# Cross attention: a finished batch's projection, norms, gate, experts and stores stand up to two slots sooner in the slot tables

## The reference

```
x = layernorm(x + self_attention(x))                       # causal, plus a "memory" term
x = layernorm(x + cross_attention(ctx, ctx, x) @ Wo.T + bo) # keys and values from ctx
x = layernorm(x + ffn(x))
# ffn: logits = x @ gate_w (8 experts), weights = softmax, top 2
#      e0 = silu(x @ w0.T + b0), e1 = silu(x @ w1.T + b1)
#      out = e0 * weight0 where expert 0 is first choice + e1 * weight1 where expert 1 is second
```

## Time and profile before

| | us |
|---|---|
| median of 3 runs | 1775.47 |
| the runs | 1770.29, 1775.82, 1775.47 |
| span of the profiled execution | 1773.4 |
| PE busy | 1681.7 (95%) |
| DVE busy | 1254.6 (71%) |
| POOL busy | 1161.8 (66%) |
| ACT busy | 974.2 (55%) |

### The profile page before, as it was taken

How to read it: one execution, slowest core, us unless ns; L and a number is a source line. 1 busy time by engine, 2 the same in 40 slices (tenths; PEclk the granted TensorE clock), 3 DMA queues, 4 the chain that set the end, 5 groups by cost and what they waited for, 6 DMA issues and landing times.

```text
span 1773.4 us, 30895 instructions
## 1 busy us (share of the span) xinstructions
PE 1681.7 (95%) x10626; PEld 1111.0 (63%) x10626; DVE 1254.6 (71%) x2785; ACT 974.2 (55%) x1939; POOL 1161.8 (66%) x964
## 2 busy tenths in 40 slices
PE   5999999999999989999998999999999999999998
PEld 4766666666666547877863556566565656656566
DVE  5677777777777666767876776877778686777745
ACT  4555555555555443433445565656666665666554
POOL 2556556556555554744565977878788786878874
PEclk9999999999999989999998999999999999999999
DMA  6556555555555464576625543535344354534210
GB/s 199 147 149 168 145 152 156 153 156 165 141 153 153 122 194 152 181 219 185 193 66 155 144 115 88 139 90 155 91 114 114 82 138 99 144 93 108 63 42 31
DMA packets 167273, 237.29 MB, mean 134 GB/s; under 512 B 22087, under 2 KB 73287, under 8 KB 167117
## 3 DMA queue, kind: packets, MB, share of 16 engines
q1 hardware_dynamic: 167116, 235.31, 48.2%
HBM read 91.57 MB, written 41.94 MB: 75 GB/s over the span
## 4 chain that ended last, share of the span: by engine, by line
PE 68%; DVE 12%; POOL 8%; DMA 4%; issue 4%; ACT 2%; SPq 1%; POOLq 0%; DVEq 0%; ACTq 0%
PE bank L1652 9%; POOL cross_added L1974 7%; PE bank L201 5%; PE bank L202 5%; PE bank L203 5%; DVE bank L585 5%; PE bank L1522 5%; PE bank L1490 5%; PE bank L1461 5%; PE bank L369 4%; PE bank L305 4%; PE bank L356 3%; DVE bank L548 2%; PE bank L1558 2%; PE bank L329 2%
## 5 line engine op out<-in xcount | busy, mean ns | idle before, releaser
L1471 DVE TENSOR_REDUCE cross_negmax<-bank 128x1 f32<-128x512 f32 x512 | 338.7, 674 | 149.8 <-PE bank L1461 147.2
L1738 ACT ACTIVATE cpt<-bank 128x512 f32<-128x512 f32 x512 | 297.7, 595 | 143.6 <-PE bank L1490 140.1
L548 DVE CUSTOM_DVE_ANT_0 bank<-bank,future 128x128 f32<-128x128 f32 (+3 forms) x512 | 243.0, 488 | 177.8 <-PE bank L356 177.7
L430 ACT ACTIVATE pt<-bank 128x256 f32<-128x256 f32 (+3 forms) x512 | 217.5, 444 | 260.2 <-PE bank L305 256.1
L1974 POOL TENSOR_TENSOR cross_added<-cross_added,cpt 128x2048 f32<-128x2048 f32 x61 | 280.0, 4591 | 11.5 <-ACT cpt L1738 11.0
L618 POOL TENSOR_SCALAR_AFFINE_SELECT pt<-pt 128x512 f32<-128x512 f32 x128 | 81.1, 634 | 246.8 <-ACT pt L430 246.8
L1490 PE MATMUL bank<-cqk 98*128 98x512 f32 x512 | 227.4, 444 | 7.1 <-ACT cpt L1738 6.2
L1461 PE MATMUL bank<-cqk 96*128 96x512 f32 x512 | 212.5, 418 | 10.7 <-DVE cross_negmax L1471 8.6
L1974 POOL TENSOR_TENSOR cross_added<-cpt,cpt 128x2048 f32<-128x2048 f32 x32 | 146.6, 4581 | 84.0 <-ACT cpt L1738 84.0
L305 PE MATMUL bank<-qk 98*128 98x256 f32 (+2 forms) x512 | 180.6, 359 | 8.4 <-ACT pt L430 3.9
L356 PE MATMUL bank<-qk 96*128 96x256 f32 (+2 forms) x512 | 169.5, 335 | 4.4 <-DMA qk<-stage 4.4
(11 more groups left out here) (207 smaller groups left out, 3623.8 us busy)
## 6 DMA issues: line engine op xcount, KB each, us to landing
qk<-stage SPq DMA_DIRECT2D x384, 128.0 KB, 2.3
cqk<-cstage SPq DMA_DIRECT2D x384, 128.0 KB, 2.3
scratch_memory<-memory SPq DMA_DIRECT2D x32, 512.0 KB, 3.8
ma<-scratch_memory SPq DMA_DIRECT2D x32, 512.0 KB, 3.9
raw<-in_x_t SPq DMA_DIRECT2D x32, 256.0 KB, 2.9
v<-in_x SPq DMA_DIRECT2D x32, 256.0 KB, 3.2
scratch_y_ar<-y_ar SPq DMA_DIRECT2D x32, 256.0 KB, 2.4
my_ar<-scratch_y_ar SPq DMA_DIRECT2D x32, 256.0 KB, 4.6
```

The costliest lines, as they stand in the source:

```text
L548: dve.tensor_tensor_reduce(out=scores, in0=scores, in1=sh.future[:, SEQ - P * (qt + 1):SEQ], scale=-1.0, scalar=-NEG, op0=ALU.add, op1=ALU ...
L1471: dve.reduce_max(s.negmax[gm % 2][:, col:col + 1], max_bank(sh, m)[:, :], AX, negate=True).then_inc(s.dve_max, 1)
L1738: act.activation(s.pt[step % 3][:, j, :], sh.bank[2 + n % 2][:, :], ACT.Exp, scale=SCALE_CROSS).then_inc(s.act_exp, 1)
```

## The change

All numbers in the slot tables from the chunk (0, 3) of the projection on become smaller by two, those of the residual loads by one or two. The chunks in slots 4 to 9 stay. The first two residual additions (slots 14 and 15, before 16 and 17) so stand in the first group of 16 slots. No instruction is added or taken away. The only effect is on where an instruction stands in its engine's list.

```diff
-PROJECT = {4: (0, 0), 5: (0, 1), 6: (0, 2), 7: (1, 0), 8: (1, 1), 9: (1, 2), 15: (0, 3), 16: (1, 3), 17: (2, 0),
-           18: (2, 1), 19: (2, 2), 20: (2, 3), 21: (3, 0), 22: (3, 1), 23: (3, 2), 24: (3, 3)}
-ADD, FACTORS, APPLY, TRANSPOSE = (16, 17, 21, 25), (18, 19, 23, 27), (20, 22, 26, 30), (24, 27, 31, 33)
-
-LOW = (29, 30, 33, 35)
-GATE, LOGITS, EXPERT = 37, 42, 44
-
-LOAD_X1 = (6, 13, 15, 21)
-
-STATS3, FACTORS3, APPLY3, STORE = (58, 64, 68, 76), (59, 65, 69, 78), (66, 71, 73, 81), (67, 72, 74, 82)
+PROJECT = {4: (0, 0), 5: (0, 1), 6: (0, 2), 7: (1, 0), 8: (1, 1), 9: (1, 2), 13: (0, 3), 14: (1, 3), 15: (2, 0),
+           16: (2, 1), 17: (2, 2), 18: (2, 3), 19: (3, 0), 20: (3, 1), 21: (3, 2), 22: (3, 3)}
+ADD, FACTORS, APPLY, TRANSPOSE = (14, 15, 19, 23), (16, 17, 21, 25), (18, 20, 24, 28), (22, 25, 29, 31)
+
+LOW = (27, 28, 31, 33)
+GATE, LOGITS, EXPERT = 35, 40, 42
+
+LOAD_X1 = (5, 11, 13, 19)
+
+STATS3, FACTORS3, APPLY3, STORE = (56, 62, 66, 74), (57, 63, 67, 76), (64, 69, 71, 79), (65, 70, 72, 80)
```

## The result

The changed kernel is slower: 1810.55 us median (1805.96 to 1811.37) against 1772.88 us (1768.87 to 1775.82) for the kernel before on the same chip, ratio 1.0212 with a 95% interval of 1.0191 to 1.0234. One of its four runs took 3162.28 us, in a slow state, and is left out of the range and the ratio; without it the median is 1809.74. The forecast was 1798.7 us with a range of 1781 to 1812 and 0.84 for slower: the direction and the range held, but the time is 12 us above the forecast and close to the upper end. As a difference to the kernel before, +23.2 us was forecast, and it is +36.2 by the spans and +37.7 by the medians.

A forecast was written before the change was run, and what follows sets the result against it. PE was taken to bound a block behind slot 36's totals, POOL's gapless additions the stretch before. +3.8 us a block (22.8 for blocks 2 to 7), +1.0 in block 1, -0.6 at the end: +23.2, 1798.7 us, range 1781 to 1812.

The forecast's parts named there:

- ACT's apply of slot 18 waits for POOL: ACT stands at k = 0's apply until POOL's factors come, four us and more, holding all exponentials behind it.
- POOL's addition of slot 23: Loses its 2.33 us wait for DVE's statistics but waits for a later exponential, starting at 1242.0 against 1238.55; net +3.45.
- The totals of slot 36: Come +3.4 us later by POOL's run or +4.2 by DVE and PE; taken as +3.8 a block.
- My second path, by DVE and PE: Totals of slot 36 through k = 3's apply in slot 28, transposes, query and two gate chunks: 1259.3, +4.2 us.
- The slower rival: DVE as bound in slots 23 and 24, apply of k = 3 holding ACT in slot 28: 1811 us, chance 0.14.
- -1.4, +0.95 and +0.45: Per block: two gate slots in PE's idle time; gate's DVE work delaying slot 43; expert matmuls leaving slots 2 and 3.
- nothing but PE counts behind the totals: From slot 36's totals to the next block's slot 7 exponential, 62.6 us, PE is busy 62.58 and alone bounds.
- The residual load: k = 3's load, behind 12 stack loads, lands about 1240.7, needed about 1242: nothing, up to +0.5 us if late.
- +1.0: Block 1's cost in us: no experts or FACTORS3 yet, so slot 20's scores can start at about 1021.65.
- 3.8 - 0.6: A full block's +3.8 us, less 0.6 at the end where a DVE instruction leaves the chain between two reciprocals.
- Faster, by the removed wait: POOL's wait at slot 23 goes, its addition starts 1.25 us sooner, plus the gate's 1.4: 1758 or 1767, chance 0.09.
- No change, absorbed: PE's 4 us already lost in slots 23 to 36 swallow the late start of 3.4: 1775, chance 0.07.

The follow-up runs named there:

- a_busy: Changed kernel with PE repeating the scores matmul in slots 19 (7 times), 26 (5) and 27 (2); 1795.66 us, ratio 1.0140 to the kernel before.
- b_gate: Kernel before with k = 3's apply, transpose and low part one slot sooner and the gate two sooner; 1779.43 us, ratio 1.0044.
- a_apply20_load: Changed kernel with applies of k = 0 and 1 in slots 20 and 21 and k = 3's residual load in slot 18; 1788.03 us, ratio 1.0097.
- a_tuned: Changed kernel with applies of k = 0, 1 at 20, 22, k = 3's load at 18, logits, experts back, last norm mostly back; 1788.14 us, ratio 1.0087.
- a_load: Changed kernel with k = 3's residual load in slot 18 instead of 19, ahead of the 12 stack loads; 1807.05 us, ratio 1.0195.
- a_apply20: Changed kernel with the applies of k = 0 and 1 in slots 20 and 21 instead of 18 and 20; 1806.16 us, ratio 1.0196.
- b_one: Kernel before with projection chunks of slots 15 to 24, additions, and factors of k = 2 and 3 one slot sooner; 1780.50 us, ratio 1.0048.
- b_one_first: Kernel of b_one with k = 3's residual load in slot 19 ahead of the stack loads, and scores repeats in slots 26, 27; 1765.32 us, ratio 0.9972.
- a_apply20_load_busy: Kernel of a_apply20_load with PE repeating the scores matmul in slots 26 (5 times) and 27 (2 times); 1777.58 us, ratio 1.0035.
- a_back: Kernel before with only the change's back half: gate, logits, experts, last norm and stores sooner; 1789.08 us, ratio 1.0102.

## Why the prediction was right, and where its size was wrong

**The mechanism, point by point.** ACT's apply of slot 18 waits for POOL: predicted four us and more, measured 3.12, since PE, and with it ACT, gets there 0.7 us later than I had it (0.6 of it is there in slot 8, whose exponential starts 1.47 us behind slot 7's against 0.85). PE's idle time ahead of slot 20's scores: predicted 2.7, measured 1.84 by the profile and 2.0 by the starts. POOL's addition of slot 23 waits for the exponential and not for DVE's statistics: so it does. Its start against slot 7: predicted +3.45, measured 28.79 less 25.22 = **+3.57**. This step, on which the forecast stood, was right to 0.1 us.

**The totals of slot 36: +3.8 predicted, +5.95 measured** (1270.83 less 9.76 less 1255.12). This is the term that was mis-sized. From the addition of slot 23 to the totals I carried 16.45 us of POOL as before and took +0.35 for the rest; it is 18.95 against 16.57, +2.38. POOL's own part held nearly to the end (6.04 us from the addition of slot 23 to that of 27 against 6.07 in before, 6.07 against 5.78 on to that of 31), but from that of 31 to the totals it is 6.84 against 4.72: POOL no longer decides there. The rest is PE's: it stands 1.47 + 0.46 us for DVE's maxima in slots 26 and 27, and then runs 3.4 us at the low clock. My second path, by DVE and PE, gave +4.2 and was the one that decided; it had neither the reciprocals with the addition of k = 3 between them nor the clock. In a_busy, where the clock stays, the totals come +4.4 (46.15 against 41.79), near that path's 4.2, and a block takes 3.8 us more than before (107.77 against 103.97), the forecast's own number, if from +4.4 and -0.6. So the step that failed in size is the clock, which was put at nothing without a reason.

The slower rival (DVE as the bound, 1811 us, chance 0.14) has the measured time and named DVE in these very slots: what happened is forecast and this rival together, not one of them. ACT's hold in slot 28, which it also names, isn't there (the apply at 1258.00 has no idle time before it), and what its DVE waits bring is in good part the clock, which neither had.

**The gate.** -1.4, +0.95 and +0.45 add up to nothing; measured from the totals to the start of slot 7's exponential is -0.67 (61.36 against 62.03; the prediction's 62.6 run to that exponential's end). The wait near slot 43 is there: 0.58 us by the profile, about 0.75 by PE's starts. But b_gate shows that PE's idle time ahead of the totals takes only some 0.4 of the 1.4 us, and that the -1.4 and the +0.95 aren't two terms. The sentence that nothing but PE counts behind the totals was wrong for slots 37 to 43, where DVE is level with PE, so a gain of PE there is given back whether or not the gate's DVE work moves.

**Slot 12 and slot 15.** The wait for the maximum behind STATS3 was predicted at 0.6 and is 0.7 by PE's starts (0.55 by the profile). The exponential of slot 15 is late as predicted, and by slot 20 nothing of it is left in a_apply20 (0.2 us): costed rightly at nothing for the path. The 0.7 of slot 12 and the 0.6 of slot 8 are another cover that the prediction didn't price: with ACT's wait gone, POOL's addition of slot 23 comes 1.4 us late in a_apply20_load (26.66 behind slot 7's exponential against 25.22), and not late in a_tuned (25.25), where the last norm, the experts and the apply of k = 1 stand back in their old slots.

**The residual load: "nothing, and up to +0.5".** Wrong in block 1, where DVE stood 3.56 us and a_load, with the load sooner, gave 4.0 us back, nearly all of the difference between +1.0 and +5.3, if with 3.4 us less of low clock in it. In the other blocks it cost nothing visible, but only under the cover of ACT's wait: a_apply20 uncovered 1.86 us. My own rule, to name the cover and what it costs without it, was kept for the chunks and not for this load. I had let it land at 1240.7 against a need at 1242. But in block 3 the 12 stack loads ahead of it start when DVE's write of what they load (L1797) has ended, and then take SP 7.8 us, as the rows of DVE's timeline and SP's queue below show; against slot 7 they start 2.7 us later than in before (18.46 against 15.76), and the residual load goes out as much later behind them.

```profile
1240.84 0.68 DVE L1797 TENSOR_TENSOR cstage<-bank,cstage 128x512 fp32r<-128x512 f32 x1
1241.55 7.77 SPq L713 DMA_DIRECT2D cqk<-cstage  x12
```

**The end and the sum.** Block 7 with the tail is +3.9 against 3.8 - 0.6, and that this is near is luck: its 10.2 us of low clock weren't forecast, and in a_busy, which has none of them, it takes 158.0 us, 0.2 less than in before. From the shift of the experts 4.7 us go from behind the last exponential to before it, which is no gain. The sum: 23.2 forecast, 5 x 1.32 more in blocks 2 to 6, 4.3 in block 1, 0.7 at the end and 1.4 ahead of block 1 make 36.2, the measured difference of the spans. That the time lies within the range is in part luck too: the range was counted from 1775.47 us, the median of three runs, and from the 1772.88 of four it would end at 1809.4, below the measured 1810.55.

**The rivals.** *Faster, by the removed wait* had decided on POOL's factors being there at slot 18, and they weren't. b_one gave it this condition (the apply stayed in slot 20): the addition of slot 23 did start 1.2 us sooner, and nothing came of it, since the factors of k = 3 waited instead (103.9 us for block 3, whose clock stayed). So it would have failed even with its condition met. The advice of the Trainium skill (Perfetto Trace Analysis, "Optimization Strategy") to interleave regimes with different bounds stands behind that rival; here it gave 0.28% at best, in b_one_first with the sooner load and the repeats, and cost 0.35 to 2.6% in every other version tried. *No change, absorbed*: PE's reserve absorbed none of it, as argued.

**What stays open.** The remaining +1.4 us a block of a_apply20_load_busy are there at POOL's addition of slot 23, behind which POOL has no gap as far as slot 31:

```profile
1236.14 4.59 POOL L1978 TENSOR_TENSOR cross_added<-cpt,cpt 128x2048 f32<-128x2048 f32 x1 [3.46 <-ACT cpt L1742]
```

This is 26.7 us behind slot 7's exponential (1209.47) against 25.2, and PE works from slot 16 to the scores of slot 23 without a wait. The two chunks more that stand ahead of them (1.4 us) don't make it late alone, since a_tuned has them too and is in time. That the 1.3 us of slots 8 and 12 do is argued from rows, as a_tuned differs from this kernel in more than the last norm. No run took DVE's work alone out of slots 23 to 26 either. And which idle time exactly brings a fall of the clock isn't known: b_one's blocks 3 and 4 have nearly the same idle times and differ in it.

## What to carry to other kernels

A wait that you can name is often the first of several that end together: a_apply20 and a_load each gained 0.2% at most, both together 1.1%. Before costing a removed or added wait, list for each later slot what is next behind it (load, other engine's queue, clock), with its slack in us, and price every cover that you use. Where a move leaves an engine idle in a loop that otherwise keeps it busy, look at the granted clock of the changed stretch too: here half the clock for 3.4 us cost more (1.3 us net) than the idle time that brought it, which in b_one's block 3 cost nothing. And a load belongs ahead of transfers in its queue that themselves wait for a compute engine.

## What the runs showed of the hardware

In all kernels here, each stretch of blocks 2 to 6 with a granted clock of 0.50 instead of 1.00 (3.4 or 6.8 us long) begins during or less than 3 us behind a PE wait of 1.4 to 4.6 us. Redundant matmuls in the waiting time (1.2 and 0.5 us of them a block, in a_busy 1.7 us more in slot 19) kept it at 1.00 in these blocks and made the kernels of a_apply20_load_busy and a_busy 0.6 and 0.7% faster than the same without. The fall is not sure for a given wait: in b_one, block 3 kept the clock and blocks 4 to 6 did not, with the same instructions, and in a_back PE stands 1.81 us in slot 35 of each of blocks 2 to 6 and the clock falls in one of them.

SP took 7.7 to 7.9 us to issue 12 DMA instructions of 128 KB one behind the other, and what stood behind them in its program went out only then.
